# A fused attention, adapter and recurrent-gate kernel: first queries spread by a head mask, first weights on two queues, finer pieces and new orders

## The reference, cut to what matters

```python
y = einsum('bnh,boh->bno', x, weight[subject_id]) + bias[subject_id]   # "condition"
q, k, v = heads of y @ Wq.T + bq, y @ Wk.T + bk, y @ Wv.T + bv         # 16 heads of 16
sim = q @ k.T / sqrt(16) / (abs(temperature) + 0.1)
scores = sum over 5 freq of alpha[h, f] * sin(2*pi * sim / freq + phi[h, f])
w = sigmoid(scores); w = w / (w.sum(-1) + 1e-10)
out = layernorm((w @ v) @ Wo.T + bo) * gamma + beta
x1 = x + out
h = relu(x1 @ W1[lang] + b1[lang])                                     # "adapter"
z = layernorm(x1 + h @ W2[lang] + b2[lang]) * gamma[lang] + beta[lang]
for t in range(32):                      # the 32 examples are the steps of a recurrence
    f, i = sigmoid(z[t] @ wf.T + c @ uf.T + bf), sigmoid(z[t] @ wi.T + c @ ui.T + bi)
    g = tanh(z[t] @ wc.T + c @ uc.T + bc)
    c = f * c + i * g
result = x1 + tanh(z @ wo.T + c @ uo.T + bo)
```

## Time and profile before

| what | value |
|---|---|
| median of 3 runs | 389.83 us (389.05 to 392.76) |
| the profiled execution's own time | 389.83 us |
| its span, first to last instruction | 388.1 us |
| mean granted TensorE clock | 0.938 |
| PE busy | 309.9 us (80%) |
| DVE busy | 298.2 us (77%) |
| ACT busy | 288.7 us (74%) |

### The profile page before, as it was taken

One profiled execution on the slowest core, in us unless ns is written; L12 is line 12 of the kernel. 1 busy time (PEld: TensorE's weight loads), 2 busy tenths in 40 slices (PEclk: granted clock), 3 DMA queues, 4 the chain that ended last, 5 costly groups with the idle time before them and its releaser, 6 DMA issues.

```text
span 388.1 us, 6640 instructions
## 1 busy us (share of the span) xinstructions
PE 309.9 (80%) x2276; PEld 174.6 (45%) x2276; DVE 298.2 (77%) x641; ACT 288.7 (74%) x422; POOL 27.9 (7%) x42
## 2 busy tenths in 40 slices
PE   4656686586488779899697797989978898888885
PEld 3435333444236445553354554546554444443333
DVE  3007678994979999889866899999999999756244
ACT  0228699978699999989959598998999988232222
POOL 6000000000010002040000001110100010001000
PEclk9986789968799999899989699999999999999999
DMA  5334646465172330005303230022031021000006
GB/s 148 114 78 107 184 109 179 113 169 202 31 209 54 74 73 1 2 0 139 55 2 52 77 90 2 2 70 52 11 84 35 2 62 49 1 2 0 0 2 216
DMA packets 31717, 27.65 MB, mean 71 GB/s; under 512 B 12227, under 2 KB 25667, under 8 KB 31684
## 3 DMA queue, kind: packets, MB, share of 16 engines
q1 hardware_dynamic: 31684, 27.23, 25.9%
HBM read 23.02 MB, written 2.10 MB: 65 GB/s over the span
## 4 chain that ended last, share of the span: by engine, by line
ACT 28%; PE 26%; DVE 16%; SPq 14%; issue 9%; DMA 5%; POOL 1%; POOLq 0%; DVEq 0%; ACTq 0%
ACT ang L912 7%; SPq L282 6%; ACT ang L903 6%; PE pg L559 5%; DVE sc L1383 4%; PE pf L406 4%; PE pf L475 2%; ACT L909 2%; ACT sc L918 2%; PE pg L552 2%; SPq L262 2%; PE pr L571 2%; DMA uout<-in_uout 2%; ACT L916 2%; DMA wc<-in_cond 2%
## 5 line engine op out<-in xcount | busy, mean ns | idle before, releaser
L1383 DVE SCALAR_TENSOR_TENSOR sc<-ang,small,sc 128x512 f32<-128x512 f32 (+1 forms) x160 | 98.6, 639 | 1.3
L912 ACT ACTIVATE ang<-ang,qs 128x2560 f32<-128x2560 int32 x32 | 77.5, 2426 | 2.9 <-DVE ang L1368 2.8
L903 ACT ACTIVATE ang<-sc,phase 128x512 int32<-128x512 f32 (+1 forms) x140 | 78.4, 625 | 1.0 <-DVE sc L1383 0.9
L559 PE MATMUL pg<-gate_u,cT 128*64 128x384 f32 x256 | 50.0, 513 | 6.7 <-DVE cT L1490 6.4
L552 PE MATMUL pg<-gate_w,zT 128*64 128x384 f32 x256 | 47.3, 492 | 2.8 <-ACT pg L940 1.6
L1368 DVE TENSOR_SCALAR ang<-ang 128x2560 int32<-128x2560 int32 x32 | 47.4, 1486 | 2.0 <-ACT ang L903 1.9
L475 PE MATMUL pf<-qm,kT 128*64 128x256 f32 x256 | 33.9, 409 | 13.6 <-issue 9.2
L944 ACT ACTIVATE gat<-pg 128x384 f32<-128x384 f32 x32 | 15.5, 483 | 30.4 <-PE pg L559 30.4
L1359 DVE TENSOR_SCALAR ang<-sc,phase 128x512 int32<-128x512 f32 (+1 forms) x60 | 24.0, 427 | 14.2 <-ACT sc L894 14.1
L475 PEld LDWEIGHTS pf<-qm,kT 128*64 128x64 f32 x256 | 18.5, 142 | 25.4 <-issue 16.7
L559 PEld LDWEIGHTS pg<-gate_u,cT 128*64 128x64 f32 x256 | 16.9, 141 | 27.5 <-issue 17.0
(11 more groups left out here) (113 smaller groups left out, 461.2 us busy)
## 6 DMA issues: line engine op xcount, KB each, us to landing
wc<-in_cond SPq DMA_DIRECT2D x32, 257.0 KB, 2.9
wa<-in_down SPq DMA_DIRECT2D x32, 66.0 KB, 1.8
w<-in_up SPq DMA_DIRECT2D x32, 64.2 KB, 2.1
xt<-in_xt SPq DMA_DIRECT2D x8, 256.0 KB, 3.2
b<-in_up_b SPq DMA_DIRECT2D x32, 64.0 KB, 2.1
out_t<-go SPq DMA_DIRECT2D x8, 256.0 KB, 2.3
xg<-in_x SPq DMA_DIRECT2D x3, 512.0 KB, 5.2
qm<-qT SPq DMA_DIRECT2D x48, 32.0 KB, 2.1
```

Of the source, the lines that this page charges most:

```text
L559: mm = pe.matmul(pg[n % 2][u * L:(u + 1) * L, 0:GCOLS], cT[:, kc, :], gate_u[:, kc, u, :], start=False, stop=(kc == KC - 1), skip_group_ch ...
L903: op = act.activation(ang[:, n % SLOTS, f, r], unit(n)[:, r], ACT.Identity, scale=TURN / FREQS[f], bias=phase[:, p * NF + f:p * NF + f + 1])
L912: act.activation(a.bitcast(F32), a, ACT.Sin, scale=2 * PI_LOW / TURN, bias=qs[:, 3:4]).then_inc(sine_ready, 1)
L1383: op = dve.scalar_tensor_tensor(out=unit(n)[:, r], in0=sine, scalar=amp, in1=unit(n)[:, r], op0=ALU.mult, op1=ALU.add)
```

## The change

The edits are:

- The eight DMAs of `spread_q(0, 0)` go. The queries of the first half of group 0 are multiplied by a 0/1 mask of each head's rows, five heads on DVE and three on ACT. The mask is one reduction of the unit matrix.
- Two of the first four `load_cond` DMAs (b = 2, 3) are issued by ACT; `small` is loaded after `xg`; ACT's table is loaded before its first wait for data.
- `ON_ACT` gives seven angles to DVE: one of unit 0, two of unit 1, one each of units 3 and 29, two of unit 31. 112 become 105.
- `condition`, `values`, `output_projection`, `output_part` and `output_kept` are called for halves of a part, `input_gates` for one kc.
- `residual`, `moments` and `modulated` are cut in two where a wait stood inside (`residual_added`, `adapted`, `shifted_language`), so that other work can stand between.
- All five order lists change. On ACT 20 loads of the table are left of 24, and one stands at the start.

```diff
-ON_ACT = [3, 4, 3, 4, 3, 4, 3, 4, 3, 4, 3, 4, 3, 4, 3, 4, 3, 4, 3, 4, 3, 4, 3, 4, 3, 4, 3, 4, 3, 4, 3, 4]
+ON_ACT = [2, 2, 3, 3, 3, 4, 3, 4, 3, 4, 3, 4, 3, 4, 3, 4, 3, 4, 3, 4, 3, 4, 3, 4, 3, 4, 3, 4, 3, 3, 3, 2]
+MASKED_BY_DVE = 5
```

```diff
 # scalar
+            act.wait_ge(ids_s, 16)
+            for j in range(1, SIZES[0] // 2):
+                for b in (2 * j, 2 * j + 1):
+                    s = act.value_load(ids[0:1, b:b + 1], min_val=0, max_val=NSUB - 1)
+                    act.dma_start(wc[:, b, :], cond_in[bass.ds(s, 1)]...).then_inc(wc_loaded[j], 16)
+            act.preload_act_table_set("silu_and_others")
+            def mask_queries():
+                act.wait_ge(q_ready, 1)
...
+                for h in range(MASKED_BY_DVE, HC):
+                    op = act.activation(qm[:, 0:nb, h % 2, h // 2, :], qT[:, 0, 0:nb * L]...,
+                                        ACT.Identity, scale=mask[:, h:h + 1])
 # vector
+            dve.wait_ge(eye_s, 16)
+            dve.tensor_reduce(mask[:, :], eye[:, :].rearrange("p (h r) -> p h r", r=HD), ..., ALU.add)
+            def mask_queries():
+                dve.wait_ge(q_ready, 1)
...
+                for h in range(MASKED_BY_DVE):
+                    op = dve.tensor_scalar(qm[:, 0:nb, h % 2, h // 2, :], qT[:, 0, 0:nb * L]...,
+                                           mask[:, h:h + 1], None, ALU.mult)
 # tensor, scores(n)
-                    pe.wait_ge(qm_loaded, (g * KC + c + 1) * 16 * HC)
+                    if n == 0:
+                        pe.wait_ge(qm_dve, 1)
+                        pe.wait_ge(qm_act, 1)
+                    wait(pe, qm_loaded, (g * KC + c) * 16 * HC)
```

More of the change, by code:

```diff
@@ L1672, in _ @@
+            cell_step(4)
+            add_sine(16, 2)
+            add_sine(16, 3)
+            state_copy(4)
             add_sine(15, 4)
-            add_sine(16, 1)
+            add_sine(16, 4)
+            base(2)
+            hidden(2)
+            angle(17, 0)
             angle(18, 0)
-            add_sine(16, 2)
-            cell_step(4)
-            add_sine(16, 3)
+            wrap(17)
+            divided(7)
+            cell_step(5)
+            adapted(2)
+            state_copy(5)
@@ L1678, in _ @@
+            angle(18, 1)
+            moments(2)
+            shifted(3)
+            wrap(18)
+            normalise(2)
             add_sine(17, 0)
-            add_sine(16, 4)
+            cell_step(6)
             add_sine(17, 1)
-            state_copy(4)
             add_sine(17, 2)
-            hidden(2)
-            add_sine(17, 3)
-            shifted(3)
-            angle(18, 1)
-            add_sine(17, 4)
-            wrap(18)
-            cell_step(5)
-            moments(2)
-            state_copy(5)
@@ L1735, in _ @@
-            residual(3)
+            angle(20, 1)
+            state_copy(8)
+            add_sine(19, 3)
+            divided(8)
+            add_sine(19, 4)
+            angle(21, 0)
+            angle(22, 0)
+            wrap(20)
+            divided(9)
+            cell_step(9)
+            angle(22, 1)
+            wrap(21)
+            values(3)
+            wrap(22)
+            add_sine(20, 0)
+            add_sine(20, 1)
+            add_sine(20, 2)
+            add_sine(20, 3)
+            state_copy(9)
@@ L1744, in _ @@
-            hidden(3)
-            cell_step(10)
-            add_sine(22, 3)
+            add_sine(21, 4)
+            state_copy(10)
+            add_sine(22, 2)
+            adapted(3)
+            angle(24, 0)
+            moments(3)
+            add_sine(22, 3)
+            angle(24, 1)
+            add_sine(22, 4)
+            normalise(3)
+            cell_step(11)
+            wrap(23)
+            wrap(24)
+            modulated(3)
+            shifted_language(3)
+            state_copy(11)
@@ L1747, in _ @@
+            conditioned(4)
+            angle(25, 0)
+            residual(4)
+            residual_added(4)
             add_sine(23, 0)
-            state_copy(10)
+            base(4)
+            cell_step(12)
             add_sine(23, 1)
-            moments(3)
+            state_copy(12)
             add_sine(23, 2)
-            add_sine(22, 4)
+            hidden(4)
             add_sine(23, 3)
-            normalise(3)
-            angle(24, 0)
-            angle(24, 1)
-            cell_step(11)
@@ L1758, in _ @@
-            wrap(24)
-            state_copy(11)
-            modulated(3)
-            residual(4)
-            angle(25, 0)
+            add_sine(24, 0)
             add_sine(23, 4)
-            divided(10)
-            add_sine(24, 0)
+            add_sine(24, 1)
             wrap(25)
-            add_sine(24, 1)
-            cell_step(12)
+            cell_step(13)
             add_sine(24, 2)
-            state_copy(12)
             angle(26, 0)
+            adapted(4)
+            angle(26, 1)
@@ L1772, in _ @@
+            state_copy(13)
+            wrap(26)
+            moments(4)
+            cell_step(14)
             add_sine(24, 3)
             add_sine(25, 0)
-            conditioned(4)
-            cell_step(13)
-            angle(26, 1)
             add_sine(24, 4)
-            state_copy(13)
-            hidden(4)
+            state_copy(14)
+            normalise(4)
             add_sine(25, 1)
-            wrap(26)
-            cell_step(14)
-            base(4)
+            divided(10)
+            modulated(4)
@@ L1809, in _ @@
-            cell_step(16)
+            divided(13)
+            angle(29, 0)
+            angle(29, 1)
+            state_copy(17)
             wrap(28)
-            angle(29, 0)
-            state_copy(16)
+            wrap(29)
             shifted(5)
-            divided(13)
+            shifted(6)
             add_sine(28, 0)
-            shifted(6)
             add_sine(28, 1)
+            cell_step(18)
+            add_sine(28, 2)
+            residual(5)
+            state_copy(18)
+            residual_added(5)
@@ L1818, in _ @@
+            add_sine(28, 3)
             values(4)
-            add_sine(28, 2)
-            cell_step(17)
-            add_sine(28, 3)
-            state_copy(17)
             add_sine(28, 4)
-            residual(5)
-            wrap(29)
+            hidden(5)
+            add_sine(29, 0)
+            base(5)
+            add_sine(29, 1)
+            adapted(5)
+            add_sine(29, 2)
+            moments(5)
+            cell_step(19)
+            add_sine(29, 3)
+            normalise(5)
```

1076 lines of the change are left out of this document (573 added, 503 removed).

## The result

The changed kernel takes 368.7 us (median of 4 runs, 368.22 to 369.79) where the kernel before takes 390.25 us on the same chip (389.05 to 392.76). The ratio is 0.9444 with a 95% interval of 0.9392 to 0.9496: 5.6% faster, some 21.5 us. The forecast was 11.2 us and 378.6 us, with a range down to 369. The profiled execution took 368.22 us, with a span of 366.4 us, against 389.83 and 388.1.

What follows compares the result with a forecast made beforehand. DVE and ACT near full in the middle were taken as the bound, then the recurrence tail. T 4.8 + 6.2 + 3.6 - 1.8 = 12.8 us earlier, less 1.6 of tail: 11.2, 389.83 to 378.6 us; range 369 to 388.

Steps and rivals of the forecast that it cites:

- Waits behind it: Behind the first boundary: three DVE waits from SP's list, 12.4 us, go; half booked, 6.2, bounds 0 and 12.4.
- the boundary's 4.8: Boundary of groups 0 and 1, 45 to 75 us: DVE 4.8 us ahead, the start's gain included; bounds 0 and 7.
- the start's 4.4: Up to the first scores: table load 1.3, mask 2.6, two issuers 0.5; 4.4 us earlier, between 2 and 6.5.
- The mask's 2.6: At the start: masked copies instead of eight spread DMAs bring the first scores 2.6 us earlier, bounds 0.6 and 3.6.
- 1.3 + 0.5: At the start: 1.3 us from the early table load, 0.5 from ACT issuing two `load_cond` (0 to 1.8).
- rival (c): At the start: constants share DMA engines with ACT's weight loads, second product up to 3.6 us later; 382.2 us, chance 0.06.
- What crosses T: Around T, the last `weights`' start (334.49 us): 3.6 us of DVE work moves behind it, 1.8 is added before.
- Tail: From T to the end: state gates 1.9 us later, 0.3 regained by output_kept; net loss 1.6, bounds 0 and 3.7.
- (b): Whole kernel: all waits vanish and ACT's relief (2.6 us) counts; 20.0 us less, 369.8 us, chance 0.18.
- (a): Middle: removed waits reappear as waits for sines or ACT, so the 6.2 us fall away; 385.5 us, chance 0.22.
- (d): Half-group boundaries: DVE waits 3.7 us each for sines in the open, up to 22 us; 397.1 us from five, chance 0.07.
- The flagged stall of load_rest(5): SP's list: load_rest(5), now behind load_rest(6) with some 11 us of issuing, named as a place that might stall.

Runs made afterwards that it cites:

- The mended queue: Kernel before with SP's new list, but load_rest(2) ahead of spread_q(2, 1) and load_rest(5) ahead of load_rest(6) and the last spreads: 0.9589.
- the late part: Kernel before with SP's list changed only from the weights of group 4 on: 0.9776.
- The four loads: Changed kernel with four ACT table loads put back, ahead of sines 7, 14, 21 and 26: 0.9489 against the kernel before.
- the constants: Kernel before with only the gate constants moved ahead of load_rest(0) on SP's list: 1.0003.
- the new order on the old lists: Kernel before with only SP's whole new list from load_cond(1, 1) on, compute orders old, first spread still by DMA: 1.0112.
- the start and the mended queue (angles as before): Kernel before with the new start and SP's new list with load_rest(2) and load_rest(5) kept early, the seven angles still on ACT: 0.9426.
- the kernel with the angles back: Changed kernel with the seven angles of units 0, 1, 3, 29 and 31 on ACT again: 0.9365 against the kernel before.
- the last variants: Changed kernel with angles back and `halved` later 0.9376; load_rest(2) and load_rest(5) earlier 0.9335; that with angles back 0.9363; all three 0.9356.

## Why the prediction was right about the sign and short in size

**The step that failed is "Waits behind it"**: it found 12.4 us of waits from SP's list, held ACT at 56 of 60 us to be next, and booked half, 6.2. The mended queue on the kernel before gained the 12.4 us in its profiled execution and about 16 us in the medians, and the late part gained 7.9 of its 8.4. The argument read a busy share as a bound. How seldom ACT holds DVE up was already in the earlier trace rows, where all waits for sines add up to 5.7 us. The four loads and the angles point the same way: 5.1 us more of ACT, spread over the middle, cost about 1.8, and 6.3 us more at both ends cost nothing, each within the intervals.

By the accounts above DVE's idle time fell by 15.6 us. The forecast implies about 6.6: 6.2 of waits and 0.4, which is the boundary's 4.8 less the start's 4.4. So 9.0 of the 10.5 us missing from the forecast (21.7 less 11.2) are idle time of DVE. Of the rest 1.5 are its work (3.35 for 1.8) and 1.1 the first angle (5.46 for 4.4), and the tail takes 1.1 back. The idle time is a balance. The three waits gave 11.9 us (12.4 less the 0.5 for `xt`) where 6.2 were booked. The sines gave 5.5 and the tokens of group 1 3.2 (4.0 less 0.8), for which nothing was booked. Longer waits for others took a part back: 2.8 us more for the product of `weighted` and 3.2 us more for ACT's angles.

**Not every wait is worth its length, though.** Single moves gave zero (the constants) or a loss (the new order on the old lists). The waits that they removed did give their length where they stood, but each move on this queue pushes something else back. The forecast's doubt was right in kind and wrong in place: where single entries were moved, what came next was a later entry of SP's queue, and even the 3.87 us, for which the list of waits names ACT, begin there.

**Start**: the first scores came 4.39 us earlier, the sum to the hundredth, and that is partly luck. In the fourteen kernels with mask and new start they begin anywhere from 19.45 to 23.39 us, in five with the old start from 25.45 to 26.10. The mask's 2.6 was 2.5, and this part repeats: from the first query half to the scores it is 4.77 us now (21.25 less 16.48) and was 7.24, and all six kernels that spread by DMA have 7.24 to 7.26, the fourteen with the mask 3.4 to 5.2. The tokens are ready for ACT 0.54 us earlier, not 1.3 + 0.5. The remaining 1.4 us lie between tokens and queries, where PE ran faster (turn 0.66 us instead of 1.12, first projections 2.87 instead of 3.58). The forecast didn't have this, and it isn't the change's: both levels occur with either start, 1.11 and 3.78 us with the start and the mended queue (angles as before), 0.66 and 3.53 with the mended queue alone. The 0.5 us for two issuers was wrong: the products begin 1.1 us later and end at 12.99 instead of 12.25. That is the case of rival (c), with a price of some 0.7 us and not 3.6. The rule of the Trainium skill (DMA: Bandwidth & Descriptors, Issuing engines are not separate DMA queues), that two issuers save only the time of issuing, agrees with this trace: 2.3 us less of issuing brought no earlier data. Which of the two issuers, the constants behind them or the later `small` delays the products was not tried apart.

**First boundary**: scores(4) at 54.6 instead of 57, and the VectorE position 7.0 us ahead (79.1 to 72.1) instead of 4.8, at its upper bound. The bubble is there: two waits of 3.27 and 1.61 us, and 1.3 us in front of two wraps, 6.2 in all where 6 or more were forecast. The 3.87 us for unit 6 come behind that position and weren't forecast, so the boundary left less than the 7.0 us.

**What crosses T**: 3.4 us less work on DVE before T where 3.6 - 1.8 = 1.8 was booked. The two amounts weren't measured apart.

**Tail**: state gates 27 begin 23.5 us behind T and those of step 28 27.2, against 20.5 and 24.2 before: 3.0 later, forecast 1.9; from step 28 to the end 29.1 instead of 29.4, the 0.3 as forecast. In all 2.7, against 1.6. The granted clock behind T was 0.97 in this execution. In the kernel with the angles back, whose lists there are the same, it was 1.00 and the tail 54.9, which is 1.3 more than before; eight more of the experiments on the changed kernel have 54.9 to 55.0. So the term was of the right size, and the rest stands beside the lower clock:

```profile
309.70:364.60 54.90, 46.96 (x274) 22.77 (x270) 28.82 (x80) 14.95 (x31) 2.77 (x6) 1.00 0.12 39
```

**The rivals.** (b), all waits vanish and ACT's relief counts, gave 369.8 us and was nearest. Its first half is shown. Its second, 2.6 us of relief for ACT, is not: of ACT's saved work the loads put back cost 1.8 us and the angles put back gained 3.1, neither clear of the intervals. (a), the waits come back, falls as the main case, though its kind is there in the 3.2 us more for ACT's angles. (d), sines in the open, falls: 0.2 us of waits for sines after. The flagged stall of load_rest(5) is real and cost some 2.7 us in the profiled execution.

**Open** are why the queue's gain is 12.4 us in the profiled execution and 16 us by the medians (that execution was the slowest of its four, 377.41 us against 374.49 to 375.97), how much of the change as given is due to its compute lists, and which of the last variants is fastest.

## What to carry to other kernels

Read a queue of DMA issues as an engine: an entry that waits for data blocks all behind it, so a new order is to be judged together with the moment at which each of its inputs is made. Two orders that differ in the place of one spread and one load_rest were worth 4% and -1% here. A high busy share of the engine in second place was no reason to halve the gain; what counts is how long the first engine waits for it in the list of waits. When an order and the lists around it were changed together, cross them two by two before crediting either.

## What the runs showed of the hardware

Splitting the first four loads of 257 KB between two issuing engines ended the issuing 2.3 us earlier and started the products 1.1 us later (9.36 against 8.25). In the five kernels with the old start the products begin at 8.05 to 8.53 us, in the fifteen with the new one at 8.70 to 10.23. The new start also loads `small` later and the constants earlier, so the split alone isn't shown to be the cause.

The 16 matmuls of the first scores took 3.02 us before, with a granted clock of 0.62, between the level of 1.2 GHz and that of 2.4, and 1.95 us after, in a stretch at 1.00. Before, PE had been idle for 3.99 us ahead of them, waiting for the spread; after, for 0.56 us. In the run without the mask it waited 3.36 us, and they took 3.68 at 0.50. All fourteen kernels with the mask waited 0.56 to 0.79 us and took 1.95. The six that spread by DMA waited 3.27 to 4.04 us, and five of them took 2.92 to 3.68; the sixth, SP's new list alone, waited 3.54 us and still took 1.95 at a clock of 1.00. So the wait was often paid a second time as slower work behind it, with 1.0 to 1.7 us, but not always.
